# Three 1 MB transfers per sequence issued by ScalarE instead of SyncE, and the largest weights taken over the partitions through DRAM and VectorE instead of on GpSimd

## What is computed

```
x = x + layernorm(attention(layernorm(x)))     # q, k, v with bias and rotary tables, causal softmax, Wo, bo
x = x + layernorm(ffn(layernorm(x)))           # silu(x @ gate * gate_s) * (x @ up * up_s) @ down * down_s, inner 1408
```

## Time and profile before

| | |
|---|---|
| Median of 3 runs | 2681.89 us (2677.47 to 2691.45) |
| The profiled execution | 2681.5 us, span 2679.8 us |
| PE busy | 2426.6 us, 91% of the span |
| DVE | 1931.4 us, 72% |
| ACT | 1446.7 us, 54% |
| POOL | 1164.6 us, 43% |
| Granted TensorE clock, mean | 0.972 |
| DMA | 305.62 MB, mean 114 GB/s |

### The profile page before, as it was taken

The page is one execution under the profiler, slowest core; times in us unless marked ns, Lnnn a source line. Parts: engine busy times, 40 slices in busy tenths (PEclk is TensorE's granted clock), DMA queues, the critical chain, the costliest instruction groups (busy, mean ns, idle before and its releaser), DMA issues. The chain is left out here.

```text
span 2679.8 us, 54601 instructions
## 1 busy us (share of the span) xinstructions
PE 2426.6 (91%) x18816; PEld 1134.6 (42%) x18816; DVE 1931.4 (72%) x5887; ACT 1446.7 (54%) x1902; POOL 1164.6 (43%) x1531
## 2 busy tenths in 40 slices
PE   4889999999999999999999973299999999999997
PEld 2434444444444444444444331144444444444443
DVE  5888889889888888988988853645555555555554
ACT  3577777777777777777777661422222222222221
POOL 3566776777776677677677642000000000000000
PEclk8899999999999999999999987699999999999999
DMA  4444445544554554554454434102111111111111
GB/s 163 120 129 141 159 144 158 168 150 151 167 159 143 166 165 145 159 168 151 143 170 142 142 103 181 72 16 79 47 47 47 63 47 47 73 52 47 47 47 48
DMA packets 178934, 305.62 MB, mean 114 GB/s; under 512 B 32416, under 2 KB 115872, under 8 KB 165536
## 3 DMA queue, kind: packets, MB, share of 16 engines
q1 hardware_dynamic: 178720, 302.86, 34.5%
HBM read 182.73 MB, written 119.01 MB: 113 GB/s over the span
## 5 line engine op out<-in xcount | busy, mean ns | idle before, releaser
L753 DVE CUSTOM_DVE_ANT_0 mx<-mx,causal 128x512 f32<-128x512 f32 (+3 forms) x2048 | 942.6, 517 | 69.7 <-PE mx L864 68.9
L587 ACT ACTIVATE probs<-ts,exp_scale 128x1024 f32<-128x1024 f32 x640 | 710.7, 1111 | 166.8 <-PE ts L878 165.8
L1153 ACT ACTIVATE silu<-gu,gate_scale 128x512 f32<-128x512 f32 x176 | 121.0, 688 | 630.9 <-PE gu L1344 630.9
L1128 POOL TENSOR_TENSOR f_rstd<-f_var,f_neg_half 128x4 f32<-128x4 f32 x32 | 32.3, 1010 | 928.7 <-DVE f_var L1271 646.0
L1294 DVE SCALAR_TENSOR_TENSOR hidden<-gu,up_scale,silu 128x512 f32<-128x512 f32 x176 | 131.9, 749 | 416.6 <-PE gu L1344 406.4
L465 POOL TENSOR_SCALAR_AFFINE_SELECT probs<-probs 128x512 f32<-128x512 f32 x512 | 336.9, 681 | 32.9 <-ACT probs L587 32.7
L892 PE MATMUL xb<-probs,vs 128*32 128x512 f32 (+3 forms) x4096 | 306.4, 440 | 13.4 <-ACT shift_rows L593 12.5
L1342 PE MATMUL gu<-f_xT_hi,gate_hi 128*128 128x512 f16 x704 | 267.7, 380 | 52.5 <-issue 52.5
L878 PE MATMUL ts<-qT,kT 64*128 64x512 f16 (+3 forms) x2048 | 246.0, 298 | 52.9 <-ACT probs L587 50.7
L753 DVE DVE_READ_ACCUMULATOR2_ANT row_max<- 128x1 f32 x2048 | 282.8, 138 | 0.0
L1344 PE MATMUL gu<-f_xT_lo,gate_hi 128*128 128x512 f16 x704 | 267.6, 380 | 0.0
(11 more groups left out here) (145 smaller groups left out, 4282.8 us busy)
## 6 DMA issues: line engine op xcount, KB each, us to landing
slots<-half SPq DMA_DIRECT2D x260, 128.0 KB, 13.7
qT<-slots SPq DMA_DIRECT2D x128, 256.0 KB, 3.6
kT<-slots SPq DMA_DIRECT2D x128, 256.0 KB, 3.7
weighed<-oT SPq DMA_DIRECT2D x128, 256.0 KB, 4.5
xn<-x SPq DMA_DIRECT2D x16, 1024.0 KB, 7.4
xr<-x SPq DMA_DIRECT2D x16, 1024.0 KB, 7.8
slots<-half SPq DMA_DIRECT2D x256, 64.0 KB
spread<-recips SPq DMA_DIRECT2D x64, 256.0 KB
```

What stands on the lines that cost most here:

```text
L587: nc.scalar.activation(probs[:, g % 2, u, :, :], ts[:, :, :], ACT.Exp, scale=exp_scale[:, 0:1]).then_inc(ts_read, 1)
L753: last = nc.vector.tensor_tensor_reduce(out=scores, in0=scores, in1=causal[:, T - P * (qt + 1):T], scale=1.0, scalar=-3e38, op0=ALU.add, o ...
```

## The change

ScalarE's program gets the three 1 MB transfers, with the same conditions: `xn` at step 9 as before, `x1` at step 15 (before 14), `xr` at step 24 (before 19), each behind all of ScalarE's other work of that step. In the setup SP writes `largest` to a small DRAM tensor `tops` (128x4), waits, and reads it back with all 512 values in every partition of `spread`; VectorE reduces these to `largest_all`. GpSimd's instruction goes; its first body starts on another condition.

```diff
@@ sync, setup
+            sp.wait_ge(largest_ready, 1)
+            sp.dma_start(tops, largest[:, 0:4]).then_inc(largest_out, 16)
+            sp.wait_ge(largest_out, 16)
+            sp.dma_start(spread[:, :], tops.rearrange("(o p) n -> o (p n)", o=1).broadcast_to([P, 4 * P])).then_inc(largest_in, 16)
@@ sync, body
-                    if s == 9 and exists(i + 2):
-                        sp.wait_ge(xT_full, NC * (i + 2))
-                        sp.dma_start(xn[:, :, :], x[i + 2, :, :, :]).then_inc(x_in, 16)
-                    if s == 14 and exists(i - 2):
-                        sp.wait_ge(x1_ready, NT * (i - 1))
-                        sp.dma_start(x1[i - 2, :, :, :], xr[:, :, :]).then_inc(x1_out, 16)
-                    if s == 19 and exists(i - 2) and exists(i - 1):
-                        sp.wait_ge(x1_out, 16 * (i - 1))
-                        sp.dma_start(xr[:, :, :], x[i - 1, :, :, :]).then_inc(xr_in, 16)
@@ gpsimd
-            pool.wait_ge(largest_ready, 1)
-            nc.gpsimd.partition_all_reduce(largest_all[:, :], largest[:, 0:4], P, RMAX).then_inc(largest_reduced, 1)
-            body(-1, (largest_reduced, 1))
+            body(-1, (offset_ready, 1))
@@ scalar, body, behind the step's other work
+                    if s == 9 and exists(i + 2):
+                        act.wait_ge(xT_full, NC * (i + 2))
+                        act.dma_start(xn[:, :, :], x[i + 2, :, :, :]).then_inc(x_in, 16)
+                    if s == 15 and exists(i - 2):
+                        act.wait_ge(x1_ready, NT * (i - 1))
+                        act.dma_start(x1[i - 2, :, :, :], xr[:, :, :]).then_inc(x1_out, 16)
+                    if s == 24 and exists(i - 2) and exists(i - 1):
+                        act.wait_ge(x1_out, 16 * (i - 1))
+                        act.dma_start(xr[:, :, :], x[i - 1, :, :, :]).then_inc(xr_in, 16)
@@ vector, scale_weights
+                dve.wait_ge(largest_in, 16)
+                nc.vector.tensor_reduce(largest_all[:, :], spread[:, :].rearrange("p (q n) -> p n q", n=4), AX.X,
+                                        ALU.max).then_inc(largest_reduced, 1)
@@ kernel
+    tops = nc.dram_tensor("tops", (P, 4), F32, kind="Internal").ap()
```

More of the change, by code:

```diff
@@ L68, in power_of_two_scales, with attention_phase @@
     link(nc.vector.tensor_scalar(unscale, power, 0.25, None, ALU.mult))
-def attention_phase(nc, x, wT, bias_row, bias_columns, rope_cos, rope_sin, slots, weighed, recips, x1):
+def attention_phase(nc, x, wT, bias_row, bias_columns, rope_cos, rope_sin, slots, weighed, recips, tops, x1):
     ctx = ExitStack()
@@ L153, in attention_phase @@
         largest_ready = sem("largest_ready")
+        largest_out = sem("largest_out")
+        largest_in = sem("largest_in")
         largest_reduced = sem("largest_reduced")
@@ L1450 @@
     recips = nc.dram_tensor("recips", (NC, P, 8 * T // P), F32, kind="Internal").ap()
+    tops = nc.dram_tensor("tops", (P, 4), F32, kind="Internal").ap()
     attention_phase(nc, ap["x"], [ap[f"w{n}T"] for n in "qkvo"], ap["bo"], ap["bias_columns"],
-                    ap["rope_cos"], ap["rope_sin"], slots, weighed, recips, x1)
+                    ap["rope_cos"], ap["rope_sin"], slots, weighed, recips, tops, x1)
     ffn_phase(nc, x1, ap["gateT"], ap["upT"], ap["downT"], ap["gate_s"], ap["up_s"], ap["down_s"], out)
```

## The result

The changed kernel takes 2704.71 us (median of 7 runs, 2692.65 to 2710.78), the kernel before 2687.24 us in the same comparison (7 runs, 2677.47 to 2691.45). The ratio is 1.0066, 95% interval 1.0048 to 1.0085: slower, by about 17.5 us. The profiled execution of the changed kernel took 2709.03 us with a span of 2707.0, 27 us over the profiled one of before; it is one of the slower ones, so its parts add up to more than the medians' 17.5.

The account below looks back on a forecast made before the run. PE was taken to bound the attention sequences (95% busy), delays of ScalarE's exponentials being paid by PE; 2681.5 + 6.1 + 4.9 - 2.9 = 2689.6 us, +0.3%, range 2674 to 2715, the forecast's own 2682 to 2697.

Parts of the forecast that it names:

- rival A: `xn` right ahead of the `slots` writes stalls every sequence, 1.9 us each over fourteen: 2713.4 us, slower; chance 0.22.
- a sign of being wrong: First scale other than 5 to 12 us later, or PE's waits in the middle stretch changing by over 10 us.
- Part 1: Setup: largest elements go through DRAM and VectorE instead of GpSimd's reduction, +6.1 us, exposed in full.
- Part 2: Three issues leave SP, 0.35 us each: 0 us, since no issue of SP ends a wait of PE.
- Part 3: Three issues come to ScalarE; the one at step 9 delays the next exponential: 14 x 0.35 = +4.9 us.
- rival B: No cost on ScalarE, issues run beside its activations, all old stalls go: 2681.9 us; chance 0.20.
- Rival D: An issue on ScalarE costs 1.2 us, 2.5 us exposed per sequence: 2720 us; chance 0.08.
- Part 4: Big transfers against small ones: half the old stalls from `xr` ahead of `slots` in sequences 8, 12, 14 regained, -2.9 us.
- Rival C: Big transfers off SP's ring: `averaged` lands 1.4 us earlier, PE's 26.8 us wait for exponentials goes: 2661 us; chance 0.07.

## Why the prediction was right or wrong

The time, 2704.71, lies within the stated range (2674 to 2715), but outside the forecast's own (2682 to 2697); it is inside the wide one because that reaches to rival A, whose pair of transfers is the wrong one, so that it holds the time is in part luck. The likeliest time, 2689.6, was 15 us short, and the class that came, slower by over 0.5%, had been given 0.35 against 0.58 for no change. Two terms are wrong and the main one has the wrong sign. The prediction had named a sign of being wrong, and it came: PE's wait for exponentials alone changed by 12.2 us, over its 10.

Part 1, the setup: +6.1 forecast, 5.9 in the trace, 7.1 timed alone. Right, also in that it is exposed whole. The pieces differ: the write let SP go on after 1.52 us (estimated 2.1), the read took 3.8 from its issue, and the reduction took 1.05 us where 0.65 had been taken. The `xn` of sequence 1 was issued at 28.90, beside the first cast and not behind all four.

Part 2, SP relieved: 0 forecast. No run tells it from that.

Part 3, the issues on ScalarE, +4.9: wrong, it is about 0 for one issue at this place. The step that failed is "what the issue takes here is paid one for one". The size was right (0.33 to 0.35 us each), but ScalarE's sequencer issues while `half` computes. PE's wait behind it was 1.51 us in sequence 7, with a GpSimd that was 0.2 us later, and 1.23 in the kernel with steps 9, 19, 29. Over sequences 1 to 13 group 1 takes 13.56 to 13.99 us in the eight kernels in which ScalarE issues `xn`, in the mean 13.73, and 13.55 to 13.89, in the mean 13.68, in the five in which SP does (the kernel with three small issues left out): 0.6 us for all 13. Three issues in a row there, though, do cost, 8.9 us by the time, 0.7 a sequence; so rival B's reason was right for one and not without bound. Rival D's 1.2 us per issue was not seen for the 1 MB transfers; the longest of the three in a row took 1.02.

Part 4, the transfers, -2.9: wrong in sign; it was +12.4. The gain that was expected is real: with `xr` gone from step 19 and on SP's queue, the kernel gains 6.4. What was missed is the step "`xr`, now at 814.4, will be some 2 to 3 us ahead of the next": the prediction looked only at what `xr` would stand ahead of. What it hurts is the `averaged` read issued a microsecond before it, and the `weighed` write between the two. On one queue a transfer 1.3 us behind costs the one ahead little (6.5 us to the product in the median of both such kernels, 5.8 without); on a second queue, 1.1 us behind or less, it runs along with it and costs 3 to 4 (9.5 in the median of the ten sequences of the changed kernel). Issued 2.1 us behind on the second queue it cost no more than on the first (6.4 to 6.7). So the loss takes both, the second queue and a distance of about a microsecond; SP's distance was never below 1.1.

The Trainium skill, DMA: Bandwidth & Descriptors, section Queues, rings and completion order, says that an engine alternates between its rings packet by packet. The prediction took that as a gain for the small transfers behind; the trace has packets of both queues in the same 7.5 us and agrees with the rule so far; the order of single packets wasn't looked into. The gain shows: with the same steps SP's wait for `slots` is 23.0 us on the second queue against 53.8 on the first. But the main effect was the other one, a loss for those ahead, 5.8 to 9.8 us in the sequence shown. The same page's section Issuing engines are not separate DMA queues says that another issuing engine saves only the sequencer's time; here the two kernels that differ by the queue of three transfers differ by some 16 to 19 us (+1.8 and about +17.5 with the pass, -6.4 and +12.4 without), so the measurement goes beyond it.

Rival A has the right mechanism: a small transfer lands late, GpSimd's or ScalarE's chain overruns its 1.3 us of spare time, the exponentials wait, one to three microseconds a time. It had the wrong pair: not `xn` at step 9 ahead of `slots`, but `xr` at step 24 behind `averaged`. `xn` on the second queue even landed faster, 4.8 us in the median against 7.4, and in none of the experiments did one issue at step 9 cost anything that can be told. SP's wait for `slots`, which A had longer, went from 55.1 to 23.0 us. A's time, 2713, is nearer than the forecast's.

Rival C, faster through an `averaged` that lands earlier, came true with other steps, in the kernels with 9, 19, 29: -14 us at best, where it had -21. Its reason holds in part: GpSimd's wait for `averaged` fell from 135.9 to 118.8 us, but PE's wait for exponentials, which it had gone whole, only from 26.8 to 21.7.

What stays open: why `xr` at step 27, where `slots` is late in both profiles, cost 13 us on one chip and 3.7 on another; whether SyncE with steps 9, 19, 29 does as well as ScalarE; and the 3 us behind the last exponential of the changed kernel's profile, which no run looked into.

## What to carry to other kernels

A transfer moved to another issuing engine's queue no longer waits for what is ahead of it, and what is ahead of it no longer goes first: look for the short transfer on a tight path that was issued about a microsecond before (here 3 to 4 us of delay; two to three microseconds before, under one). Place large transfers at the steps where no such short one is in flight; here this alone, two step numbers, turned +0.66% into -0.4%. And compare placements with each other, not with the old kernel alone: `x1` cost some 10 us at step 15, and the old kernel hid it by paying the like. One issue beside running work of ScalarE cost nothing that could be told, three in a row before a waiting engine 0.7 us a sequence.

## What the runs showed of the hardware

An issue of 1 MB on ScalarE took 0.33 to 0.35 us in the median, as on SP, and ran beside an activation that had started; three small ones in a row took 0.33 to 1.02 us each. The `xn` read of 1 MB at step 9 landed on the second queue after 4.8 us in the median against 7.4 on the first, but `xr` at step 24 after 8.1, against 7.7 at step 19 on the first, so the queue alone doesn't decide it. A write of 2 KB from 128 partitions let the waiting SP issue the next after 1.5 us. The reduction of 128x512 in a view with a stride of four elements took 1.05 us, against 2.28 for 128x2048 without one, so nearly twice as long per element; how much of that is the stride and how much the short instruction wasn't separated. The same kernel came out at 1.0049 and 1.0020 against the kernel before, on two chips, each with an interval of 0.0015 to both sides.
